# Two clips of the gate write to PSUM, and the tables that place every step of both phases are new

## The reference

```python
xe = jnp.einsum('ti,eir->ter', x, Vg)
proj = jnp.einsum('ter,eir->tei', xe, Vg)
residuals = jnp.linalg.norm(x[:, None, :] - proj, axis=-1)
rw = jax.nn.softmax(-residuals, axis=1)
mask = rw > thr                       # thr = 1/8; if no token passes anywhere, the top one
fw = rw * (mask & topk_mask)          # top 2 of 8
sw = fw.sum(axis=1, keepdims=True)
sw = jnp.where(sw == 0, jnp.ones_like(sw), sw)
w = fw / sw
```

## Time and profile before

| what | value |
|---|---|
| median of 3 runs | 1627.31 us |
| the profiled execution's own time | 1627.94 us |
| its span, first to last instruction | 1626.3 us |
| busy: TensorE, VectorE, ScalarE, GpSimd | 1481.4, 1397.2, 1242.2, 1235.5 us |
| granted TensorE clock, mean | 0.950 of full speed |
| phase one | to about 1262 us |
| one sequence in phase one's steady state | 71.8 us |
| phase two | from 1264 us to the end |

### The profile page before, as it was taken

One profiled execution on the slowest core, in us unless ns is written; L12 is line 12 of the kernel. 1 busy time (PEld: TensorE's weight loads), 2 busy tenths in 40 slices (PEclk: granted clock), 3 DMA queues, 4 the chain that ended last, 5 costly groups with the idle time before them and its releaser, 6 DMA issues.

```text
span 1626.3 us, 23772 instructions
## 1 busy us (share of the span) xinstructions
PE 1481.4 (91%) x7687; PEld 795.5 (49%) x7687; DVE 1397.2 (86%) x2518; ACT 1242.2 (76%) x2144; POOL 1235.5 (76%) x1219
## 2 busy tenths in 40 slices
PE   5356899999999999999999999999998899999997
PEld 2122344444444444444444444434444678788876
DVE  5999899999999999999999999998432688988763
ACT  6776799998989899898989989896655455455542
POOL 5988899898989889898989889898233345555552
PEclk8577799999999999999999999999999799999999
DMA  4000000000000000000000000000200000000000
GB/s 155 0 0 1 20 3 19 12 9 21 1 20 3 18 11 11 20 1 20 1 21 7 14 20 1 20 3 19 92 11 11 1 1 14 14 14 14 14 14 29
DMA packets 14688, 27.59 MB, mean 17 GB/s; under 512 B 3981, under 2 KB 4566, under 8 KB 14042
## 3 DMA queue, kind: packets, MB, share of 16 engines
q1 hardware_dynamic: 14554, 25.98, 5.7%
HBM read 9.20 MB, written 4.19 MB: 8 GB/s over the span
## 4 chain that ended last, share of the span: by engine, by line
PE 36%; POOL 24%; issue 17%; DVE 15%; ACT 7%; DMA 1%; SPq 0%; POOLq 0%; ACTq 0%; DVEq 0%
POOL sum_fast L719 9%; PE bank L1146 6%; PE bank L1639 6%; PE bank L1615 6%; DVE state_fast L695 5%; POOL prob_fast L1194 4%; PE bank L1215 3%; PE bank L808 3%; POOL sum_fast L713 2%; PE bank L1659 2%; PE bank L1588 1%; ACT prob_fast L1162 1%; PE bank L1593 1%; POOL g_prod_fast L966 1%; DVE gate_fast L859 1%
## 5 line engine op out<-in xcount | busy, mean ns | idle before, releaser
L695 DVE TENSOR_TENSOR_SCAN state_fast<-state_fast,bank 128x512 f32<-128x512 f32 x512 | 590.3, 1198 | 2.7 <-ACT bank L662 1.9
L719 POOL TENSOR_TENSOR sum_fast<-sum_fast,state_fast 128x512 f32<-128x512 f32 x384 | 481.0, 1278 | 23.4 <-DVE state_fast L695 23.4
L1162 ACT ACTIVATE prob_fast<-bank 128x1024 f32<-128x1024 f32 x320 | 325.2, 1019 | 86.1 <-PE bank L1146 63.0
L1146 PE MATMUL bank<-stacks_fast 64*128 64x512 f32 (+3 forms) x2048 | 360.8, 462 | 18.0 <-ACT prob_fast L1162 8.4
L680 ACT ACTIVATE state_fast<-chan_all_kept,neg_a_fast 128x512 f32<-128x512 f32 x512 | 341.9, 715 | 2.5 <-POOL sum_fast L713 2.1
L1146 PEld LDWEIGHTS bank<-stacks_fast 64*128 64x128 f32 x2048 | 171.9, 186 | 223.6 <-ACT prob_fast L1162 113.2
L1194 POOL TENSOR_SCALAR_AFFINE_SELECT prob_fast<-prob_fast 128x512 f32<-128x512 f32 x256 | 169.5, 676 | 131.9 <-ACT prob_fast L1162 131.8
L1215 PE MATMUL bank<-prob_fast,v_ext_fast 128*32 128x512 f32 (+3 forms) x2048 | 178.7, 461 | 2.5 <-POOL prob_fast L1194 2.4
L1828 POOL TENSOR_TENSOR cell_a_fast<-th_fast,cell_a_fast 128x512 fp32r<-128x512 f32 x64 | 90.6, 1417 | 117.4 <-ACT cell_a_fast L1700 117.2
L808 PE MATMUL bank<-we_t_fast,xnt_g_fast 128*128 128x512 f32 x256 | 139.2, 639 | 3.6 <-DVE own_fast L953 2.1
L775 PE MATMUL bank<-resid_m_fast,xnt_g_fast 128*128 128x512 f32 x256 | 130.6, 629 | 7.5 <-DVE gate_fast L859 4.9
(11 more groups left out here) (218 smaller groups left out, 2666.6 us busy)
## 6 DMA issues: line engine op xcount, KB each, us to landing
stacks_fast<-parts_fast SPq DMA_DIRECT2D x128, 64.0 KB
stacks_fast<-rest_fast SPq DMA_DIRECT2D x128, 32.0 KB
out_x<-f_out_fast SPq DMA_DIRECT2D x16, 256.0 KB, 2.0
x_res_kept<-in_x SPq DMA_DIRECT2D x1, 2048.0 KB, 13.9
chan_all_kept<-in_h_t SPq DMA_DIRECT2D x2, 1024.0 KB, 9.3
x_res_kept<-in_x SPq DMA_DIRECT2D x1, 1024.0 KB, 9.5
chan_all_kept<-in_w_t SPq DMA_DIRECT2D x3, 256.0 KB, 3.0
x_res_kept<-in_x SPq DMA_DIRECT2D x2, 256.0 KB, 2.9
```

The lines of the kernel that those rows point to most:

```text
L695: dve.tensor_tensor_scan(h[:], h[:], self.banks[0][:], 0.0, ALU.mult, ALU.add).then_inc(self.v_scan.sem)
L719: pool.tensor_tensor(part[:], part[:], self.state(b, i + 1)[:], ALU.add).then_inc(self.p_sum.sem)
L1146: ins = pe.matmul(self.scores(b, step)[:, c:c + SEQ - P * kt], rows[:, 1, h // 2, P * kt:P * kt + P], rows[:, 0, h // 2, P * kt:SEQ], star ...
L1162: act.activation(self.probs[u % 2][:, i * 1024:(i + 1) * 1024], self.scores(b, 5 * g + n)[:], ACT.Exp, scale=SCALE).then_inc(self.a_prob.sem)
```

## The change

The clip of the residual sums writes to columns 96 to 127 of PSUM bank 4 and the clip of the kept sums to columns 160 to 163; ScalarE's Ln and VectorE's reciprocal read them there. The Ln still writes `ss` in SBUF. Two more entries of `gate_room` name the places.

```diff
@@ -824,10 +824,10 @@
 
     def act_g_gate(self, b):
         act, banks = self.act, self.banks
-        ss, sp = self.gate_room()[0:2]
+        ss, sp, limited = [self.gate_room()[i] for i in (0, 1, 7)]
         yield
         act.wait_ge(self.v_g_a.sem, self.v_g_a.at(b))
-        act.activation(ss, ss, ACT.Ln).then_inc(self.a_g_norm.sem)
+        act.activation(ss, limited, ACT.Ln).then_inc(self.a_g_norm.sem)
         yield
         act.wait_ge(self.a_g_norm.sem, self.a_g_norm.at(b, 0))
         act.activation(sp, ss, ACT.Exp, scale=0.5).then_inc(self.a_g_norm.sem)
@@ -863,11 +863,11 @@
 
         sb, ps = self.gate, self.banks[4]
         by_e = lambda at, i: at[:, i:i + NT * NE].rearrange("p (k e) -> p k e", k=NT)
-        return by_e(sb, 0), by_e(ps, 0), by_e(sb, 32), by_e(ps, 32), by_e(ps, 64), by_e(sb, 96), by_e(ps, 128)
+        return by_e(sb, 0), by_e(ps, 0), by_e(sb, 32), by_e(ps, 32), by_e(ps, 64), by_e(sb, 96), by_e(ps, 128), by_e(ps, 96), ps[:, 160:160 + NT]
 
     def dve_g_gate(self, b, general):
         dve, gb = self.dve, self.gate
-        ss, sp, rw, rwp, rank, fw, kp = self.gate_room()
+        ss, sp, rw, rwp, rank, fw, kp, limited, total = self.gate_room()
         w9 = gb[:, 128:164].rearrange("p (k e) -> p k e", k=NT)
         col = lambda i: gb[:, 164 + 4 * i:168 + 4 * i]
         diff = self.banks[4][:, 256:512].rearrange("p (k e j) -> p k e j", k=NT, e=NE)
@@ -875,7 +875,7 @@
         kept = self.kept_all[:, b * NT:(b + 1) * NT]
         yield
         dve.wait_ge(self.v_g_ss.sem, self.v_g_ss.at(b, 7))
-        dve.tensor_scalar(ss, ss, LN_MIN, None, ALU.max).then_inc(self.v_g_a.sem)
+        dve.tensor_scalar(limited, ss, LN_MIN, None, ALU.max).then_inc(self.v_g_a.sem)
         yield
         dve.wait_ge(self.a_g_norm.sem, self.a_g_norm.at(b, 1))
         dve.tensor_reduce(col(0), sp, AX, ALU.min).then_inc(self.v_g_b.sem)
@@ -916,10 +916,10 @@
         dve.wait_ge(c.sem, c.at(b, 9))
         if b == 0:
             dve.wait_ge(self.p_ones.sem, self.p_ones.at(0, 2))
-        dve.tensor_scalar(col(4), kept, KEPT_MIN, None, ALU.max).then_inc(c.sem)
+        dve.tensor_scalar(total, kept, KEPT_MIN, None, ALU.max).then_inc(c.sem)
         yield
         dve.wait_ge(c.sem, c.at(b, 10))
-        dve.reciprocal(col(5), col(4)).then_inc(c.sem)
+        dve.reciprocal(col(5), total).then_inc(c.sem)
         yield
         dve.wait_ge(c.sem, c.at(b, 11))
         dve.tensor_tensor(w9[:, :, 0:NE], kp, over_e(col(5)), ALU.mult).then_inc(c.sem)
```

```diff
-PERIOD, F_PERIOD = 72390, 35011
+PERIOD, F_PERIOD = 72505, 38574
...
-    "act_g_gate": [101285, 102180, 105625, 113527, 118416],
+    "act_g_gate": [101856, 101971, 103593, 112495, 116988],
```

More of the change, by code:

```diff
@@ new lines @@
+    "act_f_rstd": [273516],
+    "act_f_turned": [-219309],
+    "act_g_gate": [101856, 101971, 103593, 112495, 116988],
+    "act_g_rstd": [73366],
+    "act_g_setup": [14899, 130390, 203327, 247960, 357890],
+    "act_g_squares": [83491, 84523, 89145, 89995, 93455, 93836, 97855, 97855],
+    "act_g_turned": [78119],
+    "act_g_xn": [75855],
+    "act_inputs": [-21576, 15981],
+    "act_nums": [239975, 255031, 263684],
+    "act_s_head": [-31445, -25221, -22615, -15001, -6829, -1357, 10108],
@@ new lines @@
+    "act_s_rstd": [-160588],
+    "act_s_turned": [-68020],
+    "act_s_xn": [-132085],
+    "act_scores": [181063, 183468, 188327, 194398, 198201, 201830, 204493, 207222, 210512, 211768, 212937, 215711,
+        219922, 224337, 234102, 237909, 242206, 243908, 246552, 250128],
+    "act_setup": [-759603, -332911],
+    "act_t_proj": [172551, 175455, 177870],
+    "act_t_rstd": [140338],
+    "act_t_setup": [35657, 91092, 142013],
+    "act_t_turned": [146858],
+    "act_t_xn": [142613],
+    "dve_bound": [84709],
@@ new lines @@
+    "dve_setup": [-215252, -195291, -171073, -39274, -18471, 25384, 27204],
+    "dve_t_norm": [142894],
+    "dve_t_out": [268558],
+    "dve_t_proj": [157572, 165014, 182544, 189255],
+    "dve_values": [246530, 248369, 261201, 261201],
+    "pe_bound": [235486],
+    "pe_f_a": [-177276, -166529, -159967, -153934],
+    "pe_f_first": [83983, 104663],
+    "pe_f_flags": [322121],
+    "pe_f_h1": [-126247, -124431, -118331, -107786],
+    "pe_f_h2": [-81386, -69445, -58316, -52290],
+    "pe_f_out": [-23484, -10157],
@@ new lines @@
+    "pe_setup": [-1342531],
+    "pe_t_out": [262205, 263858],
+    "pe_t_proj": [152804, 161416, 172560, 175089, 178370, 182685],
+    "pe_t_setup": [-17811, 32920, 85153],
+    "pe_t_turn": [145786],
+    "pe_values": [195105, 197505, 203615, 209157, 210633, 217076, 222321, 234701, 236571, 241056, 247716, 252114,
+        254117, 258059],
+    "pool_f_a": [-235005, -209018, -204617, -204617],
+    "pool_f_h1": [-173593, -161262],
+    "pool_f_h2": [-114507, -107246],
+    "pool_g_sums": [117819, 118344, 121990, 124198],
@@ L154 @@
+    "sp_loads": [-60919],
+    "sp_rows": [52313, 52313, 55084, 71467, 102253, 106915],
+    "sp_weights": [263041],
 }
 EDGES = {
[L156 to L160, removed]
```

309 lines of the change are left out of this document (133 added, 176 removed).

## The result

The changed kernel takes 1614.46 us (median of 4 runs, 1613.32 to 1615.29), the kernel before 1626.84 (4 runs, 1626.14 to 1628.66). The ratio is 0.9916, with an interval of 0.9904 to 0.9929. The kernel is faster, by 12.4 us between the medians (13.7 by the ratio). The forecast was 1594.5 in a range of 1577 to 1612: right in sign, 20 us too optimistic, and the range missed the result by 2.5 us.

What follows compares the result with a forecast made beforehand. It took the steady state, VectorE-limited in appearance, to be stopped once per sequence by the held clip L878. Terms -32.6 (L878), +0.3 (its own price), -0.5 (head), others 0, sum to -32.8: 1594.5 us, range 1577 to 1612.

Steps and rivals of the forecast that it cites:

- The mechanism of the clips: Gate clip L878, held by GpSimd's traffic, stops all four engines once per sequence; writing PSUM, it is never held.
- 183 ns: L878's own time for 32 columns with its output in PSUM, against 0.15 to 0.17 us before; 0.3 us counted.
- 11 x 2.96 = 32.6: Gain from freeing L878: eleven held clips, each period 2.96 us longer than the one without a held clip.
- L919: 0: Gain from moving clip L919 to PSUM: between 0 and 8.8 us, taken as 0, hidden in the first hold's slack.
- The order of phase one ... taken as 0: In phase one's steady state only swaps happen and each engine's work per sequence is the same, so 0 us.
- The hold moves: Rival, chance 0.04: L635 and the two L739 meet GpSimd as the clip did; 33 us lost, near 1620 to 1627.
- it never took a hold of several instructions: Argument against the rival on L635 and L739: in steady state L739 had no hold by several GpSimd instructions.
- TensorE takes over: Rival, chance 0.09: TensorE keeps 68.8 busy us plus 1.46 idle, period 70.3, gain 15.4 us, time 1612.
- 0, within 3: Phase two's new order: TensorE stays fully busy with the same instructions, one gap filled instead of another; 0 us, within 3.
- the cases above it: Rivals slower than 1612: hold moves, 1620 to 1627 (0.04); change doesn't act, 1627 (0.05); slower, 1631 and above (0.05).

Runs made afterwards that it cites:

- first: Kernel before with both clips writing PSUM and the old order in every stretch: 1590.51 us, ratio 0.9776.
- third run: Kernel before with both clips writing PSUM and only phase two in the change's order, phase one in the old order: 1588.40 us, ratio 0.9765.
- the kernel of 1651 us: Old order of phase one, clips in PSUM, phase two as in the change, with the second-half L638 moved before the scan ahead of the last L953s: 1651.27 us, 1.0142.

## Why the prediction was wrong

- **The mechanism of the clips was right.** L878 at 0.17 to 0.20 us and L919 at 0.17 in all executions, the Ln's waits down to 1.0 us in all, TensorE's busy time at 67.2 in the periods at full clock. The clip's "183 ns" came out at 182.
- **The clips' price was right, in the old order.** "11 x 2.96 = 32.6" measured 33.8 for L878 alone, "L919: 0" measured 2.6, together 36.4.
- **The step that failed is "The order of phase one ... taken as 0".** It looked at the places around the clip and at the head only, not at those around L958 and L739. It measured +24.5 us: 18.2 for L638's place, which sets L958 and L739 against GpSimd's L713 and L646 (some 4.6 of it, by the profiled executions, through TensorE's clock after the stops), and 6.3 for the rest, whose cause stays open. The steps from kernel to kernel, -36.4 (clips), -1.8 (phase two), +6.3, +18.2, make -13.7, which is the change's 0.9916; they follow one another, so that they add up proves nothing by itself.
- **The rival that was true had 0.04.** "The hold moves" named the right cause and L739, but not L958, and its price does not agree with itself: 11 x 3 = 33 is the whole gain, not two thirds of it. Measured, 20 of the forecast's 33 us went. The argument against it, "it never took a hold of several instructions", was beside the point: a hold by one instruction of 1.27 us is enough.
- **"TensorE takes over" gave 1612 and nearly the right period (70.3), for a wrong reason.** TensorE's busy time was not 68.8 but 67.2; it waited.
- **Phase two "0, within 3"** gave 2 us by the first and third run, 3.4 to 5 by the profiles.
- **The range** was cut at 1612 because the cases above it had small chances; the cost of the order was left to the rivals, and never priced from rows. The rows for it were there. This is the kernel before, in its timeline:

```profile
496.20 0.85 DVE L958 TENSOR_TENSOR x_res_kept<-own_fast,x_res_kept 128x512 f32<-128x512 f32 x1
496.48 1.72 POOL L713 TENSOR_TENSOR sum_fast<-state_fast 128x512 f32<-128x512 f32 x1
498.16 0.66 DVE L638 TENSOR_SCALAR chan_all_kept<-bank 128x512 f32<-128x512 f32 x1
```

L958 has a lead of 0.28 us over its neighbour, and the new list puts 0.66 us ahead of it. These rows give the risk, not its size: the other engines' lists were new too.

## What to carry to other kernels

When a change frees one instruction from a meeting with another engine and also brings a new order, price the two apart: list every instruction of the same kind (here VectorE operations with two SBUF inputs, and a tensor_scalar from SBUF to SBUF), read how far each starts from its neighbour on the other engine, and ask which of those margins is smaller than what is moved ahead of it. The margin was 0.28 us in the old lists and 0.08 in the new ones, the moved instruction took 0.66, and its place was worth 18 us here, half of what the clips gave. A hold costs time only where it lies on the path that sets the period, and there no more than its length less the waits that it covers, so measure from a fixed mark to the end of the operation that the bound engine waits for.

## What the runs showed of the hardware

- A VectorE operation on 128x512 with two SBUF inputs that starts 0.01 to 0.57 us behind a GpSimd instruction ends 0.55 us after that one does (L958 at 494.23, L739 at 497.08, 494.00 and 486.71). If it starts ahead, GpSimd's is the longer one, 1.72 to 1.75 us for 1.27 (L713 at 484.46 and 488.52). "SBUF — State Buffer" in the Trainium skill (section "Who interferes with whom") says that whoever comes first has the shared pair for its whole instruction; these rows agree. Where the two start within a few hundredths, the recorded order does not tell who wins: 497.07 and 639.23 above, and in the kernel of 1651 us L958 starts at 656.65, 0.02 us ahead of L646, and takes 1.83 us.
- The small clip L878 behaved otherwise in the kernel before: it was blocked over three ends of GpSimd instructions, the wide operations for 1.86 us at most, one whole GpSimd instruction. No run here tells why.
- The mask L1194, which reads a single tensor, holds L739 too: 1.16 us behind a mask of 0.63.
- A tensor_scalar that reads SBUF and writes PSUM was never held: L878 and L919, 32 of 32 executions in the change, and 0.20 us at most in every other kernel with both clips in PSUM.
- TensorE's clock fell to 0.55 after one stop of 1.7 us and stayed at 1.00 after others as long (3 falls in 11 in the change); each fall cost 1.60 us.
